# Two graph attention layers: an epilogue of 13 operations, and the score products of layer 0 issued by VectorE in place of GpSimd

## The reference, cut to what matters

```
for layer 0 (x: 4096 x 64, adj: 4096 x 4096 int32, symmetric, diagonal set):
    e   = leaky_relu(s[:, None] + t[None, :], 0.2),   s = (x W0) a_first,  t = (E W0) a_second
    att = softmax(where(adj > 0, e, -inf))
    x1  = layernorm(x + elu(att @ E + x))
for layer 1:
    wh  = x1 W1,   e = leaky_relu(s + t, 0.01),   s = wh a_first,  t = wh a_second
    x2  = layernorm(x1 + softmax(where(adj > 0, e, -inf)) @ wh + bias)
```

## Time and profile before

| | us |
|---|---|
| median of 3 runs | 660.34 (659.3 to 661.42) |
| the profiled execution | 659.63 |
| its span, first to last instruction | 657.8 |

### The profile page before, as it was taken

How to read it: one execution, slowest core, us unless ns; L and a number is a source line. 1 busy time by engine, 2 the same in 40 slices (tenths; PEclk the granted TensorE clock), 3 DMA queues, 4 the chain that set the end, 5 groups by cost and what they waited for, 6 DMA issues and landing times.

```text
span 657.8 us, 14211 instructions
## 1 busy us (share of the span) xinstructions
PE 517.0 (79%) x6034; PEld 230.6 (35%) x6035; DVE 567.6 (86%) x727; ACT 516.8 (79%) x593; POOL 188.1 (29%) x144
## 2 busy tenths in 40 slices
PE   1305779899989899999988428779887898899894
PEld 1203335334444334444444212233333233333341
DVE  3898988999899898888467889989998998899685
ACT  0856998899999996988676318979997899699673
POOL 0110000198027850673083000003301450332240
PEclk9999999999999899999999757999999999999997
DMA  7899885777477737330200000000000001000000
GB/s 156 326 352 338 292 298 207 273 255 251 158 259 275 249 119 288 130 130 2 73 2 19 1 33 1 1 33 1 1 10 33 1 1 33 1 1 18 1 17 9
DMA packets 18631, 76.46 MB, mean 116 GB/s; under 512 B 6552, under 2 KB 8776, under 8 KB 10376
## 3 DMA queue, kind: packets, MB, share of 16 engines
q1 hardware_dynamic: 17560, 74.63, 32.5%
q0 software_dynamic: 256, 0.80, 0.5%
q10 hardware_dynamic: 752, 0.13, 0.1%
HBM read 74.47 MB, written 1.09 MB: 115 GB/s over the span
## 4 chain that ended last, share of the span: by engine, by line
PE 28%; DVE 23%; ACT 21%; issue 18%; DMA 5%; POOL 4%; SPq 1%; POOLq 0%; ACTq 0%; DVEq 0%
ACT Pm L620 15%; PE acc L940 15%; DVE junk L726 11%; PE zps L983 8%; DVE zps L820 8%; DMA adj_in<-in_adj 5%; PE acc L947 4%; ACT zps L612 2%; ACT v L513 2%; SPq L354 1%; POOL tAB L412 1%; ACT u_row L529 1%; DVE tot L761 0%; POOL rstd L471 0%; POOL o L409 0%
## 5 line engine op out<-in xcount | busy, mean ns | idle before, releaser
L620 ACT ACTIVATE Pm<-zps,ebias 128x1024 f32<-128x1024 f32 (+1 forms) x320 | 293.4, 933 | 77.0 <-DVE zps L820 67.9
L726 DVE CUSTOM_DVE_ANT_0 junk<-v,u_row 128x2048 int8<-128x2048 int8 (+3 forms) x136 | 305.4, 2266 | 3.3 <-ACT v L513 3.2
L983 PE MATMUL zps<-D,v 128*128 128x128 bf16 x2048 | 173.7, 225 | 55.8 <-DVE D L748 28.7
L983 PEld LDWEIGHTS zps<-D,v 128*128 128x128 fp8e4 x2048 | 118.8, 99 | 216.5 <-ACT zps L612 92.0
L820 DVE SCALAR_TENSOR_TENSOR zps<-S_row,tau_col,zps 128x1024 f32<-128x1024 f32 (+1 forms) x135 | 141.2, 1052 | 52.4 <-PE zps L983 49.6
L612 ACT ACTIVATE zps<-S_row,ntau_col 128x1024 f32<-128x1024 f32 (+1 forms) x185 | 177.4, 959 | 5.4
L940 PE MATMUL acc<-Pm,X 128*32 128x512 f32 (+2 forms) x1280 | 146.5, 530 | 21.4 <-ACT Pm L620 18.1
L940 PE MATMUL acc<-Pm,VE 128*32 128x512 f32 (+2 forms) x1280 | 147.9, 535 | 15.7 <-ACT Pm L620 7.8
L402 POOL TENSOR_TENSOR tAB<-flag,totW 128x520 f32<-128x520 f32 (+1 forms) x8 | 11.1, 1388 | 300.8 <-ACT totW L539 160.9
L947 PE MATMUL acc<-Pm,ones 128*32 128x256 f32 (+1 forms) x1280 | 87.5, 346 | 0.0
L947 PEld LDWEIGHTS acc<-Pm,ones 128*32 128x32 f32 x1280 | 43.3, 114 | 71.4 <-issue 62.0
(11 more groups left out here) (145 smaller groups left out, 277.8 us busy)
## 6 DMA issues: line engine op xcount, KB each, us to landing
adj_in<-in_adj SPq DMA_DIRECT2D x64, 1024.0 KB, 6.2
S_row<-S_rows_scratch SPq DMA_DIRECT2D x5, 512.0 KB, 3.8
S_row<-S_rows_scratch SPq DMA_DIRECT2D x3, 256.0 KB, 3.2
u_row<-u_row_scratch SPq DMA_DIRECT2D x3, 256.0 KB, 3.5
out<-tAB SPq DMA_DIRECT2D x3, 256.0 KB, 2.6
S_row<-S_rows_scratch POOLq DMA_DIRECT2D x1, 512.0 KB, 10.7
S_row<-S_rows_scratch POOLq DMA_DIRECT2D x1, 256.0 KB, 7.5
out<-tAB SPq DMA_DIRECT2D x2, 128.0 KB, 2.0
```

Of the source, the lines that this page charges most:

```text
L620: a.activation(Pm[:, k % PB, 0:R(C) * P], zps[:, buf("step", k), 0:R(C) * P], ACT.Exp, bias=ebias[:, int(seeded(k)), J:J + 1])\
L726: d.tensor_tensor_reduce(out=junk[:, at % 2, 0:cols.stop - cols.start], in0=v_bytes[:, rt, cols], in1=u_row[:, cols], scale=1.0, scalar=-3 ...
L983: last = t.matmul(zps[:, buf("step", k), r * P:(r + 1) * P], v[:, chunks[C][1] + r, J * P:(J + 1) * P], D[:, C % 2, r, :], start=(r * P % ...
```

## The change

1. **Layer 0, ELU.** The minimum on GpSimd goes. ScalarE computes relu(-y) and then exp(-relu(-y)) at the place of the old single exponential, and GpSimd adds the relu to y. The -1 of the ELU goes too, since the layer norm removes it (L420).
2. **Layer 1, bias.** The bias is put into a row of the projection's weights `W1p`, so the operation L425 goes, with its broadcast load. `W1d`, a second copy of the weights, goes as well.
3. **Small scalings.** The mean's (L429) and the variance's (L470) go from GpSimd to VectorE, right behind the sums, in both layers.
4. **Score products.** L438 and L439 are issued by VectorE inside `scores(C)` for chunks 0 to 3. For these `scores` and `rows` stand at J = 22 and 25 in place of 24 and 26; in chunk 4 they stay at 21 and 22.

So GpSimd is left with 11 operations in an epilogue of layer 0 and 9 in one of layer 1.

```diff
-    AFTER_WIDE = dict(elu=11, sums=14, squares=18, scores=24, rows=26)
+    AFTER_WIDE = dict(elu=11, sums=14, squares=18, scores=22, rows=25)
...
-            link(ns.tensor_tensor(tBf, h, xs, ALU.add))
             if layer(C) == 0:
-                ns.tensor_scalar(tAf, tBf, 0.0, -3.0e38, ALU.min, ALU.max).then_inc(min_done, 1)
-                eng.wait_ge(min_done, C + 1)
-                link(ns.tensor_tensor(tBf, tBf, tAf, ALU.subtract))
+                ns.tensor_tensor(tBf, h, xs, ALU.add).then_inc(elu_in, 1)
+                eng.wait_ge(negative_done, C + 1)
+                link(ns.tensor_tensor(tBf, tBf, tAf, ALU.add))
                 link(ns.tensor_tensor(tBf, tBf, xs, ALU.add))
                 eng.wait_ge(elu_done, C + 1)
-                link(ns.tensor_scalar(h, h, 1.0, -1.0, ALU.mult, ALU.add))
                 ns.tensor_tensor(tBf, tBf, h, ALU.add).then_inc(y_done, 1)
             else:
-                if C == NC:
-                    eng.wait_ge(b_loaded, 16)
-                ns.tensor_tensor(tBf, tBf, per_feature(bias_bc[:, :]), ALU.add).then_inc(y_done, 1)
+                ns.tensor_tensor(tBf, h, xs, ALU.add).then_inc(y_done, 1)
             if C in LASTS:
                 sums(C)
-            eng.wait_ge(tot1_done, C + 1)
-            link(ns.tensor_scalar(mean[:, 0:n], tot1[:, 0:n], -1.0 / F, 0.0, ALU.mult, ALU.add))
+            eng.wait_ge(mean_done, C + 1)
             link(ns.tensor_tensor(tBf, tBf, per_row(mean[:, 0:n]), ALU.add))
             ns.tensor_tensor(tAf, tBf, tBf, ALU.mult).then_inc(sq_done, 1)
             (squares if C in LASTS else inverse)(C)
             eng.wait_ge(rstd_done, C + 1)
             ns.tensor_tensor(xs if layer(C) == 0 else tBf, tBf, per_row(rstd[:, 0:n]), ALU.mult).then_inc(new_done, 1)
-            if layer(C) == 0:
+            if layer(C) == 0 and C == NC - 1:
                 eng.wait_ge(new_done, C + 1)
                 ns.tensor_tensor(tAf, xs, per_feature(wbc[:, 2, :]), ALU.mult).then_inc(sprod_done, 1)
                 ns.tensor_tensor(tBf, xs, per_feature(wbc[:, 3, :]), ALU.mult).then_inc(tprod_done, 1)
...
             def inverse(C):
-                pool.wait_ge(tot2_done, C + 1)
-                link(g.tensor_scalar(var[:, 0:R(C)], tot2[:, 0:R(C)], 1.0 / F, LN_EPS, ALU.mult, ALU.add))
+                pool.wait_ge(var_done, C + 1)
...
-            act.dma_start(W1d[F:2 * F, :], W1).then_inc(W1d_loaded, 16)
             for half in range(2):
                 act.dma_start(W1p[half * F:half * F + F - 1, half * F1:half * F1 + F], W1[1:F, :])\
                     .then_inc(W1p_loaded, 16)
+                act.dma_start(W1p[half * F + F - 1:half * F + F, half * F1:half * F1 + F],
+                              bias.rearrange("(one f) -> one f", one=1)).then_inc(W1p_loaded, 16)
             act.dma_start(W1_first[:, :], W1[0:1, :].broadcast_to([P, F])).then_inc(W1p_loaded, 16)
-            act.dma_start(bias_bc[:, :], bias.rearrange("(one f) -> one f", one=1).broadcast_to([P, F]))\
-                .then_inc(b_loaded, 16)
...
             def elu_exp(C):
-                act.wait_ge(min_done, C + 1)
-                a.activation(o[:, 0:R(C), 0:F], tA[:, 0:R(C), 0:F], ACT.Exp).then_inc(elu_done, 1)
+                act.wait_ge(elu_in, C + 1)
+                a.activation(tA[:, 0:R(C), 0:F], tB[:, 0:R(C), :], ACT.Relu, scale=-1.0).then_inc(negative_done, 1)
+                act.wait_ge(negative_done, C + 1)
+                a.activation(o[:, 0:R(C), 0:F], tA[:, 0:R(C), 0:F], ACT.Exp, scale=-1.0).then_inc(elu_done, 1)
...
             def sums(C):
                 dve.wait_ge(y_done, C + 1)
-                d.tensor_reduce(tot1[:, 0:R(C)], tB[:, 0:R(C), :], AX.X, ALU.add).then_inc(tot1_done, 1)
+                link(d.tensor_reduce(tot1[:, 0:R(C)], tB[:, 0:R(C), :], AX.X, ALU.add))
+                d.tensor_scalar(mean[:, 0:R(C)], tot1[:, 0:R(C)], -1.0 / F, None, ALU.mult).then_inc(mean_done, 1)
 
             def squares(C):
                 dve.wait_ge(sq_done, C + 1)
-                d.tensor_reduce(tot2[:, 0:R(C)], tA[:, 0:R(C), 0:F], AX.X, ALU.add).then_inc(tot2_done, 1)
+                link(d.tensor_reduce(tot2[:, 0:R(C)], tA[:, 0:R(C), 0:F], AX.X, ALU.add))
+                d.tensor_scalar(var[:, 0:R(C)], tot2[:, 0:R(C)], 1.0 / F, LN_EPS, ALU.mult, ALU.add)\
+                    .then_inc(var_done, 1)
 
             def scores(C):
                 xc = xcols(C)
+                if C < NC - 1:
+                    xs = X[:, xc, 0:F]
+                    per_feature = [wbc[:, k, :].unsqueeze(1).broadcast_to([P, R(C), F]) for k in (2, 3)]
+                    dve.wait_ge(new_done, C + 1)
+                    d.tensor_tensor(tA[:, 0:R(C), 0:F], xs, per_feature[0], ALU.mult).then_inc(sprod_done, 1)
+                    d.tensor_tensor(tB[:, 0:R(C), :], xs, per_feature[1], ALU.mult).then_inc(tprod_done, 1)
...
             def totals_W(l):
                 pe.wait_ge(totrep_saved, l + 1)
                 wait_buf(pe, "totals W", l)
-                t.matmul(zps[:, buf("totals W", l), 0:F], totrep, (identf, W1d)[l][F:2 * F, -F:],
+                if l:
+                    pe.wait_ge(W1p_done, 2)
+                t.matmul(zps[:, buf("totals W", l), 0:F], totrep, (identf[F:2 * F, F:2 * F], W1p[F:2 * F, F1:F1 + F])[l],
```

More of the change, by code:

```diff
@@ L97, in build @@
         wbc = sb("wbc", [P, 4, F])
-        bias_bc = sb("bias_bc", [P, F])
-        W1d = sb("W1d", [P, F])
         W1p = sb("W1p", [P, 2 * F1])
@@ L145, in build @@
         acc = ctx.enter_context(nc.psum_tensor("acc", [P, 2, BANK], F32))
-        w_loaded, b_loaded, e_loaded, x_loaded = sem("w_loaded"), sem("b_loaded"), sem("e_loaded"), sem("x_loaded")
+        w_loaded, e_loaded, x_loaded = sem("w_loaded"), sem("e_loaded"), sem("x_loaded")
         adj_landed = [sem(f"adj_landed{b}") for b in range(AB)]
@@ L156, in build @@
         wbc_done, wbc_saved, pick_done = sem("wbc_done"), sem("wbc_saved"), sem("pick_done")
-        W1d_loaded, W1p_loaded, W1p_done = sem("W1d_loaded"), sem("W1p_loaded"), sem("W1p_done")
+        W1p_loaded, W1p_done = sem("W1p_loaded"), sem("W1p_done")
         S_first_written = sem("S_first_written")
@@ L174, in build @@
         acc_saved, proj_done, o_saved = sem("acc_saved"), sem("proj_done"), sem("o_saved")
-        flag_added, rden_done, min_done, elu_done = sem("flag_added"), sem("rden_done"), sem("min_done"), sem("elu_done")
-        y_done, tot1_done, sq_done, tot2_done = sem("y_done"), sem("tot1_done"), sem("sq_done"), sem("tot2_done")
+        flag_added, rden_done, elu_in = sem("flag_added"), sem("rden_done"), sem("elu_in")
+        negative_done, elu_done = sem("negative_done"), sem("elu_done")
+        y_done, mean_done, sq_done, var_done = sem("y_done"), sem("mean_done"), sem("sq_done"), sem("var_done")
         rstd_done, new_done = sem("rstd_done"), sem("new_done")
@@ L479, in _ @@
             pool.wait_ge(memsets, 5)
-            pool.wait_ge(W1p_loaded, 48)
+            pool.wait_ge(W1p_loaded, 80)
             for half in range(2):
@@ L964, in _ @@
             pe.wait_ge(pick_done, 1)
-            pe.wait_ge(W1d_loaded, 16)
             pe.wait_ge(u_saved, JT // GT)
```

## The result

| | before | changed |
|---|---|---|
| median us | 659.99 (6 runs, 659.3 to 661.42) | 663.30 (6 runs, 661.96 to 664.41) |
| profiled execution, its span | 659.63, 657.8 | 663.27, 661.5 |
| ratio, 95% interval | | 1.0045 (1.0033 to 1.0056) |

What follows compares the result with a forecast made beforehand. ScalarE was taken to pace chunks 1 and 2, TensorE 3 and 4, VectorE leading chunk 7. Chunks 1 to 4 +1.1, layer 1 -1.3, bare parts -0.8: together -1.0, 659.3 us by the median, range 655.9 to 662.4.

Steps and rivals of the forecast that it cites:

- the new places: J = 22 and 25 in the wide chunks: three steps of about 2 us for 3 us of work, costed at nothing.
- The relu: ScalarE's added operation, 0.62 us wide: +0.7 in chunk 2, -0.8 in chunk 1 where a 1.25 us wait goes.
- The products: Two on VectorE in `scores`, 0.68 us each: covered in chunks 1 and 2, +0.2 in chunk 3, +0.5 in chunk 4.
- The +0.4 of the relu: Chunk 4: GpSimd's additions wait for the relu, y comes later, and TensorE's stall of 1.89 us grows by 0.4.
- The epilogue in layer 0 and the scalings: Layer 0's relu and product terms; scalings on VectorE +0.1 in chunk 4, +0.8 in 6 and 7, +0.4 in 8 and 9.
- -0.1 - 0.2 bare: Bare epilogues: -0.1 after chunk 4 for minimum and scaling against relu wait, -0.2 for the variance moved to VectorE.
- +1.0 of chunk 4: Chunk 4's terms: 0.4 for the wait on the relu, 0.5 for the products, 0.1 for the scalings.
- The bias: L425 gone from layer 1: -2.0 in chunk 7, -0.5 in chunk 6, 0 in chunk 8, -0.5 after chunk 9.
- A: Relief worth more: chunks 1 and 2 gain what VectorE nets, 2.1 us in chunk 2, some 1.3 in 1; 656.0, chance 0.25.
- B: Chunk 4's two stalls grow by 2 and 1.5 us, chunk 3's block costs 1; +2.4, 662.7, chance 0.10.
- C: VectorE becomes the bound: no relief, 1.8 us per chunk bare in chunks 1 and 2; +2.6, 662.9, chance 0.06.
- D: Layer 1's relief doesn't come, as GpSimd's remaining operations meet maxima in place of L425; +1.0, 661.3, chance 0.17.

Runs made afterwards that it cites:

- e2: The kernel before with only the places changed, scores at J = 22 and rows at 25, products still on GpSimd: 663.36 us, ratio 1.0054.
- e6: The changed kernel, places 22 and 25 kept, with one seed of chunk 3 moved from step 24 to step 23: 660.35 us, ratio 1.0000.
- e5: The changed kernel with rows back at J = 26 and scores staying at J = 22: 660.39 us, ratio 1.0005.
- e1: The changed kernel with scores and rows back at J = 24 and 26, products staying on VectorE: 660.26 us, ratio 1.0004.
- e10: The changed kernel, places 22 and 25 kept, with one seed of chunk 3 moved from step 25 to step 26: 661.74 us, ratio 1.0015.
- e4: The changed kernel with places back at 24 and 26 and products back on GpSimd, so the new epilogue alone: 660.86 us, ratio 1.0011.
- e7: The changed kernel with places back at 24 and 26 and layer 1's bias (L425) added on GpSimd again: 662.11 us, ratio 1.0027.
- e9: The changed kernel with scores back at J = 24 and rows staying at 25: 662.58 us, ratio 1.0030.
- e3: The kernel before with only the two products of chunks 0 to 3 moved to VectorE, old places and epilogue: 660.63 us, ratio 1.0007.

## Why the prediction was wrong, point by point

**The step that failed** is the sentence on the new places, which "leave three steps of about 2 us for 3 us of work, one more than before" and which stand in the sum at nothing ("I cost this at nothing"). I asked whether the inputs are ready at the new places, and not what stands behind them. Three things changed together in chunk 3: VectorE's block moved from ahead of two seeded steps (24 and 25) to ahead of one (22), so step 23 comes late; with rows at 25 the seed of step 25 can't overtake it; and the seeds moved so that 26 and 27 both need VectorE. Measured: 3.0 us (663.30 against 660.26), and 3.2 with the old epilogue (e2), there in part in the chunks 1 and 2. Either repair suffices, the first of the three (e6) or the second and third together (e5): chunk 3 then takes 65.9 us, where e1 has 65.1. e10, which takes the second and third away in another way, keeps half of the loss, and how the 3 us divide among the three stays open. The slack of 11 us that I read off for VectorE in chunk 3 is a mean; at one step it was none.

**The relu.** Right. ScalarE's pair takes 0.62 and 0.63 us and the hand-over to itself 0.03, and in chunk 1 (0.41 and 0.42) it starts without the wait of 1.25 us. That chunk 1 gained 0.4 and not 0.8 goes with a new wait of 1.03 us for VectorE at step 27, which the new places left unseeded:

```profile
136.44 0.41 ACT L571 ACTIVATE tAB<-tAB 128x256 f32<-128x256 f32 x1
136.88 0.42 ACT L573 ACTIVATE o<-tAB 128x256 f32<-128x256 f32 x1
...
173.25 1.11 ACT L613 ACTIVATE Pm<-zps,ebias 128x1024 f32<-128x1024 f32 x1 [1.03 <-DVE zps L822]
...
208.09 0.62 ACT L571 ACTIVATE tAB<-tAB 128x512 f32<-128x512 f32 x1
208.74 0.63 ACT L573 ACTIVATE o<-tAB 128x512 f32<-128x512 f32 x1
```

The prediction read one wait of ScalarE in chunk 1 of the kernel before; there is a second, 0.48 us for a part of the adjacency at 180.74, which changes nothing in the sum.

**The products.** 0.68 us each, as taken, in the groups by form:

```profile
L766 DVE TENSOR_TENSOR tAB<-X,wbc 128x512 f32<-128x512 f32 x3 | 2.0, 683 | 0.0
```

Their +0.2 in chunk 3 was right at the old places (e1: 65.1 for 65.0), and their +0.5 in chunk 4 too high: TensorE waits 1.85 us where it waited 2.01. The +0.4 of the relu there didn't come either: y is ready 0.4 us later in the chunk, as forecast, and VectorE waits 2.33 us for it (before 1.78), but TensorE's stall behind it is 1.82 us (before 1.89). With one low stretch in it, chunk 4 takes 43.8 us in the kernel before and 43.7 to 43.8 in e4, e5, e7 and e9.

**The epilogue in layer 0 and the scalings** together, with the products' part, I had at +2.0: 0.7 - 0.8 + 0.2 + 1.0 in the chunks of layer 0, 1.2 for the scalings in layer 1, and -0.1 - 0.2 bare. e7, which has all of these and L425 still, is 1.7 us over the kernel before (0.8 to 2.7 by its interval). The sum is right in size, though half of it stands on the +1.0 of chunk 4 that the traces don't have; that the rest makes up for it is luck.

**The bias** I had at -2.0 - 0.5 in the chunks and -0.5 at the end: -3.0. By the medians of e7 against e5 and e6 it is -1.7, known to about 1 us. In chunk 7 the two long maxima became one (the other lies beside L412 and stays), but another, at 531.94, now lies beside GpSimd's square (L426) and takes 3.12 us, so four maxima over 2.5 us are still four, and VectorE is busy for 59.75 us where it was 59.76:

```profile
531.94 3.12 DVE L719 CUSTOM_DVE_ANT_0 junk<-v,u_row 128x2048 int8<-128x2048 int8 x1
```

What chunk 7 lost instead is a wait of VectorE for TensorE, in the kernel before 1.34 us long and right behind the low stretch at 524.5 us. VectorE's waits in the chunk fall with it from 3.7 to 2.3 us, and this accounts for the 1.3 us:

```profile
527.71 1.29 DVE L820 SCALAR_TENSOR_TENSOR zps<-S_row,tau_col,zps 128x1024 f32<-128x1024 f32 x1 [1.34 <-PE zps L983]
```

So chunk 7 came near my number, but not by my mechanism. Whether L425 brings the low stretch there or only goes with it was not tested. By e7 the whole term is mis-sized by some 1.3 us. With the places this would make up the distance, -1.0 + 3.0 + 1.3 = +3.3, but the intervals of e1 and e7 are as wide as the term, so the fit is agreement, not proof. It would also account for 1.3 of the 2.5 us by which e4 lies over its sum; the rest of e4, 1.2 us, stays open (its interval reaches 0.9 us to either side).

**The rivals.** A is false: chunks 1 and 2 didn't gain what VectorE nets. VectorE nets less, too: the conversions and maxima next to GpSimd's remaining operations still take 2.06 to 3.26 us, 8 of them in chunk 2, where there were 11, and what they take over the medians falls from 9.2 to 7.2 us, by 2.0 and not 2.8. B had the right sign and nearly the time, by luck, as it had the wrong place: chunk 4's stalls are as before, and what I called a block ahead of unseeded steps in chunk 3 I had priced at 1 us. C is false, TensorE doesn't wait for `D` at the start of chunk 2 or 3. D holds for chunk 7, where the long maxima are as many as before. The warning of the Trainium skill (Perfetto Trace Analysis, Optimizing Scalar/DVE Operations) that work moved between these two engines may not help fits e3, where the move is worth nothing either way (ratio 1.0007); its first half, that a saturated engine is to be relieved, isn't contradicted, but going against it cost nothing here, since ScalarE leads in chunks 1 and 2.

## What to carry to other kernels

When a block of operations of an in-order engine is moved along a schedule, read the next operations behind its new place on that engine and who waits for them, not only whether its inputs are there. Where buffers rotate over several kinds of users, moving one user by a step shifts who follows whom in every later buffer, and a planner may pick other steps; print the plan before and after, and compare it. A cheap first experiment is the move of the place alone, in the old kernel.

## What was not expected of the hardware

The stretches at 1.2 GHz move with the program. The kernel before has one at 524.5 us in chunk 7, the changed kernel and e1 have it in chunk 8 (at about 576 and 574), and each time chunk 8 is 1.9 us longer, while chunk 7, in which VectorE leads, is 1.3 us shorter without it. In the changed kernel TensorE had stood 2.23 us just before, and in chunk 3, too, a low stretch (from about 310 us) follows TensorE's stall of 2.26 us. The kernel before has the stall in chunk 8 as well (2.22 us), and no low stretch there. What decides was not tested. The profiled executions hold none, one or two of them in the chunks 3 and 4. Chunk 4 shows their price: it takes 42.8 us with none (changed, e6), 43.7 to 43.8 with one (e4, e5, e7, e9) and 45.2 to 45.3 with two (e10, e1), so 1.0 to 1.5 us apiece. A difference under 2 us is better read from medians.

The last column but two of the windows shows the clock, as a share of 2.4 GHz, in the two stretches of the changed kernel, chunk 8 and chunk 3:

```profile
575.90:579.30 3.40, 3.40 (x24) 0.97 (x16) 1.15 (x1) 2.85 (x3) 1.13 (x1) 0.54 0.01 2
309.60:313.00 3.40, 3.40 (x26) 1.09 (x27) 0.00 (x0) 3.20 (x5) 0.00 (x0) 0.55 0.01 2
```
